# A four-layer graph network on one core: the split of the mask multiplies between GpSimd and VectorE goes from 4:4 to 5:3

## The reference

```python
logits  = q @ k.T / sqrt(32)
# layer of clipped adjacency: softmax(logits + log(max(adj, 1e-8)))
# layer of biased adjacency:  softmax(logits + 2*adj - 1) * (0.25 + 0.75*adj), normalised again
attended = weights @ v
```

## Time and profile before

| | |
|---|---|
| median of 3 runs | 4772.2 us |
| the profiled execution | 4770.82 us, its span 4769.0 us |
| TensorE matmuls busy | 4307.2 us (90%) |
| VectorE busy | 3509.2 us (74%) |
| GpSimd busy | 1895.1 us (40%) |
| ScalarE busy | 2024.3 us (42%) |
| mean granted TensorE clock | 0.934 of full speed |

### The profile page before, as it was taken

The page is one execution under the profiler, slowest core; times in us unless marked ns, Lnnn a source line. Parts: engine busy times, 40 slices in busy tenths (PEclk is TensorE's granted clock), DMA queues, the critical chain, the costliest instruction groups (busy, mean ns, idle before and its releaser), DMA issues.

```text
span 4769.0 us, 60615 instructions
## 1 busy us (share of the span) xinstructions
PE 4307.2 (90%) x16432; PEld 2005.4 (42%) x16432; DVE 3509.2 (74%) x4722; ACT 2024.3 (42%) x3638; POOL 1895.1 (40%) x1064
## 2 busy tenths in 40 slices
PE   7998899988999889998899898998989989899898
PEld 5523264232743337432374323743237332463324
DVE  3798748987489864898648986488855888558893
ACT  3264432544335443354423644235442354424543
POOL 1164602646026450264502645036440365404553
PEclk9998999989999899998999999999999999999999
DMA  3201102011020110201101011110111101111010
GB/s 104 67 18 32 49 23 59 18 32 49 25 59 16 34 47 28 56 16 34 47 32 53 15 34 47 33 53 14 36 47 34 49 14 36 49 36 47 14 35 16
DMA packets 109021, 179.63 MB, mean 38 GB/s; under 512 B 28256, under 2 KB 51040, under 8 KB 108704
## 3 DMA queue, kind: packets, MB, share of 16 engines
q1 hardware_dynamic: 108704, 175.89, 12.8%
HBM read 83.12 MB, written 8.39 MB: 19 GB/s over the span
## 4 chain that ended last, share of the span: by engine, by line
PE 59%; issue 17%; POOL 14%; DVE 7%; ACT 2%; POOLq 0%; DMA 0%; SPq 0%; DVEq 0%; ACTq 0%
PE ps L618 11%; PE ps L514 11%; POOL region_p L1324 9%; PE ps L560 9%; PE ps L506 8%; PE ps L597 6%; PE ps L584 6%; PE ps L707 5%; PE ps L550 2%; DVE row_max L1063 2%; POOL rstd L1336 1%; POOL v_head L1318 1%; DVE region_p L1055 1%; DVE sums_t L1034 1%; POOL y_t L1389 1%
## 5 line engine op out<-in xcount | busy, mean ns | idle before, releaser
L1324 POOL TENSOR_TENSOR region_p<-region_p,mask 128x1024 f32<-128x1024 f32 x512 | 1303.5, 2547 | 733.8 <-ACT region_p L827 733.6
L827 ACT ACTIVATE region_p<-ps 128x512 f32<-128x512 f32 x2048 | 1111.3, 595 | 907.8 <-PE ps L584 905.5
L1063 DVE TENSOR_REDUCE row_max<-ps 128x1 f32<-128x1024 f32 x1024 | 1213.5, 1214 | 42.7 <-PE ps L597 41.6
L618 PE MATMUL ps<-region_p,v_head 128*64 128x512 f32 x4096 | 1132.9, 634 | 74.4 <-POOL region_p L1324 30.2
L1055 DVE TENSOR_TENSOR region_p<-region_p,mask 128x1024 f32<-128x1024 f32 x512 | 767.3, 1501 | 67.3 <-ACT region_p L827 66.3
L597 PE MATMUL ps<-region_k,region_q 96*128 (+1 forms) x2048 | 659.2, 411 | 57.8 <-DVE row_max L1063 53.1
L584 PE MATMUL ps<-region_q,region_k 97*128 (+1 forms) x2048 | 657.1, 401 | 3.7 <-ACT region_p L827 1.1
L560 PE MATMUL ps<-values,region_k 128*128 128x256 f32 x2048 | 475.7, 387 | 0.0
L1336 POOL TENSOR_TENSOR rstd<-var_eps,minus_half 128x2 f32<-128x2 f32 (+1 forms) x160 | 119.5, 747 | 880.1 <-DVE var_eps L1015 880.1
L597 PEld LDWEIGHTS ps<-region_k,region_q 96*128 (+1 forms) x2048 | 130.1, 100 | 723.4 <-issue 459.6
L618 PEld LDWEIGHTS ps<-region_p,v_head 128*64 128x64 f32 x4096 | 208.9, 138 | 520.2 <-issue 393.4
(11 more groups left out here) (148 smaller groups left out, 4493.6 us busy)
## 6 DMA issues: line engine op xcount, KB each, us to landing
mask<-in_adj SPq DMA_DIRECT2D x64, 512.0 KB, 7.8
mask<-in_adj_t SPq DMA_DIRECT2D x64, 512.0 KB, 3.2
y_t<-o_raw SPq DMA_DIRECT2D x256, 64.0 KB, 2.0
sums_t<-o_raw SPq DMA_DIRECT2D x256, 64.0 KB, 2.0
region_q<-region_p SPq DMA_DIRECT2D x192, 64.0 KB, 2.0
region_k<-region_p SPq DMA_DIRECT2D x192, 64.0 KB, 2.0
region_q<-sums_t SPq DMA_DIRECT2D x192, 64.0 KB, 2.0
region_k<-sums_t SPq DMA_DIRECT2D x192, 64.0 KB, 2.0
```

What stands on the lines that cost most here:

```text
L618: last = nc.tensor.matmul(ps[64 * c:64 * c + 64, 6 + i, :], v_head[i][:, t, :], probs[:, t % RING, c * HALF:(c + 1) * HALF], start=(t == 0 ...
L827: nc.scalar.activation(probs[:, t % RING, c * HALF:(c + 1) * HALF], ps[:, 4 + c, :], ACT.Exp, scale=DK ** -0.5).then_inc(exp_done, 1)
L1063: nc.vector.tensor_reduce(row_max[i][:, t:t + 1], flat[:, (t % 2) * N:(t % 2 + 1) * N], AX.X, ALU.max)\
L1324: nc.gpsimd.tensor_tensor(p, p, mask[:, t, :], ALU.mult).then_inc(masked_pool, 1)
```

## The change

One table of numbers is changed, and with it DVE_TILES, which becomes (1, 4, 6).

```diff
-POOL_TILES = (1, 3, 5, 7)
+POOL_TILES = (0, 2, 3, 5, 7)
 DVE_TILES = tuple(t for t in range(T) if t not in POOL_TILES)
```

## The result

The changed kernel takes 4801.7 us, the median of 10 runs (4780.8 to 4804.3), against 4772.1 us before (10 runs, 4769.1 to 4773.2). The ratio is 1.0055, with a 95% interval of 1.0045 to 1.0066. It is slower, as forecast, by 29.6 us where 20.8 was forecast, and inside the range. The profiled execution took 4802.3 us, with a span of 4800.5 against 4769.0.

The account below looks back on a forecast made before the run. TensorE bounds heads 0 to 5, and the exclusion between VectorE's and GpSimd's two-input products bounds heads 6 and 7. 8 x 2.2 + 8 x 0.4 = 20.8 us slower gave 4793 us, range 4772 to 4818.

Parts of the forecast that it names:

- What bounds the kernel: TensorE sets the pace in heads 0 to 5; in heads 6 and 7 the mask multiplies of VectorE and GpSimd matter.
- the steady heads: Heads 0 to 5 of a pass, 96 in all, where TensorE works 16.20 of 16.30 us.
- the door: What two-input products of VectorE and GpSimd pass one at a time: 1.08 us for VectorE, 2.22 us for GpSimd.
- Steady heads cost nothing: Heads 0 to 5 lose nothing: GpSimd's three pieces in a row need 5.2 us, leaving 1.7 us spare at tile 3.
- Layer 0, +2.2 us a pass: In heads 6 and 7 of layer 0, the last multiply ends at 35.6 us instead of 33.4.
- The walk: Hand-stepped schedule of heads 6 and 7; each piece starts when its engine, its exponential and the door allow.
- Layer 1, 2.3 - 2.6 + 0.7 = +0.4 us a pass: Heads 6 and 7 of layer 1: 2.3 us later at full clock, less 2.6 us slow clock before, plus 0.7 after.
- The 0.7: Layer 1: us a pass still lost to TensorE's lower clock after the change, taken between 0 and 2.6.
- the slow stretch: Head 7 of layer 1: TensorE at its lower clock (1.2 of 2.4 GHz) after a 2.47 us wait, costing 2.6 us before.
- The sum: Whole kernel: 8 x 2.2 + 8 x 0.4 = 20.8 us slower.
- The tail hides nothing of it: End of layer 0's heads: TensorE waited 3.39 us for the last multiply, so the full 2.2 us a pass counts.
- The busy times: Whole kernel: GpSimd's busy time rises 301 us and more; VectorE's falls by about 155 us or less.

Follow-up runs that it names:

- the two runs with additions: Changed kernel plus two unread two-input products, or two unread reciprocals, on VectorE in head 7 of layer 1: 4805.2 us and 4781.4 us.

## Why the prediction was right, and where it was off

- **What bounds the kernel.** Right. TensorE sets the steady heads, and the door sets heads 6 and 7. The run with the steady heads alone (1.0004) and the one with heads 6 and 7 alone (1.0052) separate them, and taking work from the door in heads 6 and 7 gave 0.9794.
- **The door and its prices.** Right. VectorE's products and masks with two inputs and GpSimd's multiplies exclude each other, at about 1.1 and 2.2 us; a reciprocal doesn't take part. The lock that the Trainium skill describes on SBUF — State Buffer, "SBUF: two separate sides", agrees with what the two runs with additions show.
- **Steady heads cost nothing.** Right, tile 3 included: ready 5.1 us after tile 2's exponential, where I had 5.2, and taken at 6.87.
- **Layer 0, +2.2 us a pass.** Right in six of eight graphs (the last multiply ends at 35.6 us, as walked, where it was 33.4), 4.1 and 4.2 in the other two. The walk took the order at the door as given by the prices alone. The run with head 6 alone showed that this was luck in part: a tenth of a microsecond between VectorE's mask and GpSimd's tile 5 is worth 2.6 us.
- **Layer 1, 2.3 - 2.6 + 0.7 = +0.4 us a pass.** The 2.3 and the places of the waits, tiles 0, 3 and 5, were right (the last multiply ends at 31.2 us, as walked; the two longest waits are 1.74 and 1.67, where I had 1.8). The 0.7 was mis-sized: the slow stretch vanished, the lower end of the bounds, and a pass got 0.4 us shorter (131.7 to 131.2). Even where one fell there, it cost head 7 nothing: with the clock at 0.91 in the run with heads 6 and 7 alone, second graph, and at 0.92 with the reciprocals, head 7 took 20.1 us as well. That is 8 x (0.4 + 0.4) = 6 us less than forecast.
- **The sum.** Here a term was missing. I costed nothing outside the heads, and 12.3 us of the 31.5 lie there. The step that failed is "The tail hides nothing of it": the end of layer 0's heads moved by 2.2 us, and I took what follows as moved by the same 2.2. It came 3.6 us later at the first exponential of layer 1; as far as the rows show, because TensorE's slow stretches fell on other matmuls. In the sum of the heads alone I was 1.5 us off, and that is luck in part: layer 0 was 4.2 us above its share (21.8 against 17.6) and layer 1 5.7 below (-2.5 against 3.2).
- **The busy times.** GpSimd's multiplies rose by 311 us as I said (301 and more), but its total by 208, since I had overlooked that its copy would no longer be held out. VectorE's multiplies fell by 92 us and its total by 70, within "155 or less": the multiplies and masks that stayed are held out for longer.

## What to carry to other kernels

Where two engines share elementwise work, count what their instructions hold of anything they exclude each other from, not only each engine's busy time: here a multiply was "cheap" on an engine that was idle 60% of the time, and cost 1.1 us of a shared resource that was full. Look for such a resource in the instructions that are much longer than their shortest, and check who ended just before them. A split that is free in one stage can be wrong in another, so choose it by stage. And judge a change in a stage by that stage's own rows: the change cost the heads 19 us here, and what lies outside them differed by 12 to 38 us between runs that have the same code there.

## What the runs showed that I had not expected

- **A local change is not repeated as it is.** +1.8 us a graph in the heads became +3.3 us over the graph, and the same changed code ran in 4781 to 4804 us, where the kernel before kept within 4 us in the 10 runs beside it (in the 23 beside the experiments it ran in 4762.8 to 4776.3). The cause read from the rows, but not tested, is where TensorE's lower clock falls: on eight matmuls that take 5.20 us instead of 3.70, or on ones that have time.
- **The order at the door.** Two requests 0.1 us apart, in the one order or the other, moved the end of a pass by 2.6 us, as two graphs of one run show, through a wait on a third engine: ScalarE waited 1.65 us for a mask before it could make the next exponential.
- **Work that cost nothing in its head changed the total by 20 us.** Adding two reciprocals to the changed kernel left its head 7 as it was, and the run took 4781.4 us. That is one run, and it lies within the spread of the changed kernel's own.
